# First keys' half of group 1 stored and loaded apart, slot by slot over two queues; first queries and constant rows over GpSimd's queue

## The reference

```
proj = quant4(x) @ ternary(Wqkv).T + b         # one projection for q, k and v
q = proj as (token, head, 16);  k = v = proj as (head, token, 16)
q, k = rotary(q), rotary(k)
ql, kl = q @ U, k @ U                          # U is 16 x 32
y  = softmax(ql @ kl.T / 4) @ v
x  = layernorm(x + quant4(y) @ ternary(Wo).T)
h  = silu(x @ w1.T * s1) * (x @ w2.T * s2)     # 256 -> 1024
h  = gelu(h @ h1.T * hs1);  h = gelu(h @ h2.T * hs2)
out = layernorm(x + h @ w3.T * s3)
```

## Time and profile before

| | |
|---|---|
| median of 3 runs | 2631.76 us |
| the profiled execution's own time | 2628.7 us |
| its span, first to last instruction | 2626.8 us |
| TensorE busy (matmul) | 2517.5 us, 96% |
| ScalarE busy | 2018.0 us, 77% |
| VectorE busy | 1735.6 us, 66% |
| GpSimd busy | 32.3 us, 1% |
| mean granted TensorE clock | 0.985 of full speed |
| DMA: moved, mean rate | 172.34 MB, 66 GB/s |
| first scores of attention start | 77.67 us |

### The profile page before, as it was taken

How to read it: one execution, slowest core, us unless ns; L and a number is a source line. 1 busy time by engine, 2 the same in 40 slices (tenths; PEclk the granted TensorE clock), 3 DMA queues, 4 the chain that set the end, 5 groups by cost and what they waited for, 6 DMA issues and landing times.

```text
span 2626.8 us, 41383 instructions
## 1 busy us (share of the span) xinstructions
PE 2517.5 (96%) x15898; PEld 1095.5 (42%) x15898; DVE 1735.6 (66%) x2465; ACT 2018.0 (77%) x2234; POOL 32.3 (1%) x64
## 2 busy tenths in 40 slices
PE   3799999999999999999999999999959999999998
PEld 2232222222222222222222222222238888888886
DVE  7354335887788788777877877877244656556563
ACT  2799999999999999999999999999932222222232
POOL 0000001200000000000000000000100000000000
PEclk8899999999999999999999999999979999999999
DMA  3544448833343333333333434323610001110000
GB/s 103 97 104 95 110 110 167 166 64 69 60 78 66 72 69 58 73 73 65 65 70 58 77 67 72 67 60 70 121 44 9 19 6 24 24 24 8 16 8 17
DMA packets 99992, 172.34 MB, mean 66 GB/s; under 512 B 30897, under 2 KB 56529, under 8 KB 99809
## 3 DMA queue, kind: packets, MB, share of 16 engines
q1 hardware_dynamic: 89304, 151.88, 28.8%
q0 software_dynamic: 8640, 15.73, 3.0%
q10 hardware_dynamic: 1864, 2.28, 0.4%
HBM read 144.34 MB, written 25.49 MB: 65 GB/s over the span
## 4 chain that ended last, share of the span: by engine, by line
PE 82%; ACT 7%; issue 5%; DVE 3%; DMA 2%; SPq 1%; ACTq 0%; DVEq 0%; POOLq 0%
PE PS L697 31%; PE PS L667 22%; PE PS L1052 18%; ACT PB L745 6%; PE PS L1037 5%; PE PS L1064 2%; PE PS L682 2%; ACT EXP L745 1%; PE PS L456 1%; PE PS L452 1%; DMA KSL<-KSD 0%; DVE yq L781 0%; DVE same L783 0%; DMA wh1r<-in_mlp 0%; PE PS L1026 0%
## 5 line engine op out<-in xcount | busy, mean ns | idle before, releaser
L745 ACT ACTIVATE PB<-PS 128x1024 f32<-128x1024 f32 x1856 | 1735.1, 1156 | 47.2 <-PE PS L667 44.4
L697 PE MATMUL PS<-PB,V 128*17 128x512 f32 x7424 | 977.8, 598 | 2.8 <-DVE accS L810 1.8
L667 PE MATMUL PS<-QSL,KSL 49*128 49x512 f32 x3904 | 840.5, 470 | 31.6 <-DMA KSL<-KSD 18.3
L667 PEld LDWEIGHTS PS<-QSL,KSL 49*128 49x128 f32 x3904 | 352.1, 184 | 951.5 <-ACT PB L745 856.0
L768 DVE SCALAR_TENSOR_TENSOR EXP<-EXP 128x1024 f32<-128x1024 f32 x288 | 352.8, 1225 | 9.9
L1127 ACT ACTIVATE hfr<-PS,s 128x512 f32<-128x512 f32 x128 | 86.8, 689 | 300.5 <-PE PS L1052 300.4
L697 PEld LDWEIGHTS PS<-PB,V 128*17 128x17 f32 x7424 | 123.1, 95 | 281.9 <-issue 217.2
L1052 PE MATMUL PS<-hidden_ar,wh1r 128*128 128x512 f32 x1024 | 237.5, 391 | 0.0
L756 DVE TENSOR_SCALAR EXP<-PS 128x512 f32<-128x512 f32 x192 | 132.6, 691 | 157.3 <-PE PS L682 154.9
L1052 PE MATMUL PS<-hidden_br,wh2r 128*128 128x512 f32 x1024 | 235.3, 390 | 0.0
L1052 PEld LDWEIGHTS PS<-hidden_br,wh2r 128*128 128x128 f32 x1024 | 191.7, 188 | 39.4
(11 more groups left out here) (149 smaller groups left out, 1455.9 us busy)
## 6 DMA issues: line engine op xcount, KB each, us to landing
KSL<-KSD SPq DMA_DIRECT2D x254, 256.0 KB
KSL<-KSD SPq DMA_DIRECT2D x254, 128.0 KB
QSL<-QSD SPq DMA_DIRECT2D x64, 132.0 KB
QSD<-qhl SPq DMA_DIRECT2D x32, 256.0 KB
wh2r<-in_mlp POOLq DMA_DIRECT2D x32, 256.0 KB, 4.3
KSD<-khl SPq DMA_DIRECT2D x60, 128.0 KB
xg<-in_x SPq DMA_DIRECT2D x8, 512.0 KB, 6.7
QSL<-QSD SPq DMA_DIRECT2D x64, 64.0 KB
```

The source lines that it names most:

```text
L667: ins = pe.matmul(PS[:, 2 * (pair % SLOTS) + e, :], KSL[r, q % 2, s, k * P:(k + 1) * P], QSL[r, b % 2, s, :], start=True, stop=True, tile_ ...
L697: ins = pe.matmul(ACC[i * VW:i * VW + DK + 1, :], V17[:, HT * h + u, c, :], probs[:, (i % 2) * QW:(i % 2 + 1) * QW], start=kt == 0, stop=k ...
L745: act.activation(probs, PS[:, slot:slot + 2, :].rearrange("p a b -> p (a b)"), ACT.Exp).then_inc(at["probs_ready"], 1)
```

## The change

It splits the first half of group 1's keys (keys 0 to 2047 of its two heads, which pieces 0 and 1 need) from the rest. It has a semaphore of its own, `k_first`. SP and ScalarE each store their part of this half, wait for all four of these stores, load their `e` of piece 0, store their part of the second half, and load their `e` of piece 1. So each slot is now filled by both queues, where before SP filled slot 0 and ScalarE slot 1. GpSimd loads the first queries, stores the constant rows of block 0, waits for them and loads the constants of both slots. The first scores of the two first pieces wait for `consts_first`, the first for `q_first`, and the counts on `k_in` and `q_in` are lowered to match. SP's load of piece 2 waits for the second half's stores as well.

```diff
         def first_scores_pe(pe, at, pair):
...
             if s == 0 and k == 0:
                 pe.wait_ge(at["k_in"][q % 2], keys_in(at, 0, q))
-            if s == 0 and kt == 0:
-                pe.wait_ge(at["q_in"][b % 2], (b // 2 + 1) * 64)
+                if q < 2:
+                    pe.wait_ge(consts_first[q], 32)
+            if unit == 0 and s == 0:
+                pe.wait_ge(q_first, 64)
+            elif s == 0 and kt == 0:
+                pe.wait_ge(at["q_in"][b % 2], (b // 2 + b % 2) * 64)
...
+        def keys_stored(eng, g):
+            if g == 1:
+                eng.wait_ge(k_first, 64)
+            eng.wait_ge(k_out[g], 64 if g == 1 else 128)
...
-        def store_keys(eng, g, p):
+        def store_keys(eng, g, p, halves=(0, 1)):
-            for half in range(2):
+            for half in halves:
                 for u in range(2):
                     eng.dma_start(KSD[2 * g + u, (1 - p) * DK:(2 - p) * DK, half * (N // 2):(half + 1) * (N // 2)].rearrange(
-                        "f (c k) -> c f k", c=8), khl[:, p, half, u * 256:(u + 1) * 256].bitcast(F32)).then_inc(k_out[g], 16)
+                        "f (c k) -> c f k", c=8), khl[:, p, half, u * 256:(u + 1) * 256].bitcast(F32)).then_inc(
+                            k_first if (g, half) == (1, 0) else k_out[g], 16)
...
-                for p in range(int(g == 1), 2):
-                    store_keys(sp, g, p)
+                if g == 1:
+                    store_keys(sp, g, 1, (0,))
+                else:
+                    for p in range(2):
+                        store_keys(sp, g, p)
...
+        def first_keys(eng, e):
+            eng.wait_ge(k_out[0], 128)
+            eng.wait_ge(k_first, 64)
+            load_keys(eng, first, 0, (e,))
+            store_keys(eng, 1, 1 - e, (1,))
+            load_keys(eng, first, 1, (e,))
...
         def _(sp):
...
                 if v == (KG, 1, 1):
-                    sp.wait_ge(q_out[0], 64)
-                    sp.wait_ge(qn_out[0], 16)
-                    load_queries(sp, first, 0, 0)
-                if v == (KM, 0, 1):
-                    sp.wait_ge(consts_out[0], 16)
-                    load_consts(sp, first, 0)
-                    for g in range(2):
-                        sp.wait_ge(k_out[g], 128)
-                    load_keys(sp, first, 0)
+                    first_keys(sp, 0)
...
         def _(pool):
+            pool.wait_ge(q_out[0], 64)
+            pool.wait_ge(qn_out[0], 16)
+            load_queries(pool, first, 0, 0, q_first)
+            pool.wait_ge(consts_ready, 1)
+            store_consts(pool, 0)
+            pool.wait_ge(consts_out[0], 16)
+            for q in range(2):
+                load_consts(pool, q, consts_first[q])
...
         def _(act):
...
                 if v == (KG, 1, 1):
-                    store_keys(act, 1, 0)
-            act.wait_ge(consts_out[0], 16)
-            load_consts(act, first, 1)
-            for g in range(2):
-                act.wait_ge(k_out[g], 128)
-            load_keys(act, first, 1)
+                    store_keys(act, 1, 0, (0,))
+                    first_keys(act, 1)
```

More of the change, by code:

```diff
@@ L238, in postln_block @@
         consts_ready, dve_s = sem("consts_ready"), sem("dve_s")
+        k_first, q_first, consts_first = sem("k_first"), sem("q_first"), [sem(f"consts_first{k}") for k in range(2)]
         q_out, k_out = [sem(f"q_out{g}") for g in range(NQ)], [sem(f"k_out{g}") for g in range(NQ)]
@@ L303, in keys_in @@
             if at is first:
-                return b * 160 + (96 if k < 2 else 160)
+                return b * 160 + (96 if k < 2 else 160) - 32
             return n0 * (QPB * 32) + (q // 2 + 1) * 64
@@ L371, in postln_block, with load_keys @@
         y_rows = a["y"].rearrange("(n r) (q c) -> n (r q) c", n=NB_ALL, c=H * DK)
-        def load_keys(sp, at, q):
+        def load_keys(sp, at, q, rows=(0, 1)):
             hb, k = divmod(q % (NBLK * QPB), QPB)
             ks = KSD.rearrange("(s e) r k -> e r s k", e=2)
-            for e in range(2):
+            for e in rows:
                 for r0, r1, to in ((0, 2 * DK, 0), (DK, 2 * DK, 2 * DK)):
@@ L465, in setup_pe, with stored_before @@
             ins.then_inc(setup_full, 1)
+        def keys_stored(eng, g):
+            if g == 1:
+                eng.wait_ge(k_first, 64)
+            eng.wait_ge(k_out[g], 64 if g == 1 else 128)
+        def stored_before(eng, what, g):
+            if what == KG:
+                keys_stored(eng, g - 1)
+            else:
+                eng.wait_ge(q_out[g - 1], 64)
         def setup_act(act, what, i, g):
@@ L481, in setup_act @@
                 else:
-                    hl, high, out, count = (khl, k_high, k_out, 128) if what == KG else (qhl, q_high, q_out, 64)
+                    hl, high = (khl, k_high) if what == KG else (qhl, q_high)
                     if i == 0 and g:
-                        act.wait_ge(out[g - 1], count)
+                        stored_before(act, what, g)
                     act.copy(hl[:, 0, i, :], bank).then_inc(high, 1)
@@ L585, in setup_dve @@
             elif what in (KG, QT_):
-                hl, high, out, count = (khl, k_high, k_out, 128) if what == KG else (qhl, q_high, q_out, 64)
+                hl, high = (khl, k_high) if what == KG else (qhl, q_high)
                 v.wait_ge(setup_full, use + 1)
                 if i == 0 and g:
-                    v.wait_ge(out[g - 1], count)
+                    stored_before(v, what, g)
                     v.wait_ge(k_abs if what == KG else q_abs, g)
@@ L647, in store_setup, with store_consts @@
                 b = g // 2
+                if b == 0:
+                    return
                 sp.wait_ge(consts_ready, b + 1)
[L649 to L650 removed]
+                store_consts(sp, b)
+        def store_consts(eng, b):
+            eng.dma_start(KSD[BL * b:BL * b + BL, 2 * DK:2 * DK + 1, 0:KEYS].rearrange("h a k -> (h a) k"),
+                          kcr[BL * b:BL * b + BL, :].bitcast(F32)).then_inc(consts_out[b], 16)
         x_rows = a["x"].rearrange("(t p) d -> p t d", p=P)
```

18 lines of the change are left out of this document (10 added, 8 removed).

## The result

The changed kernel takes 2620.94 us (median of 6 runs, 2618.33 to 2622.76) against 2630.53 us (6 runs, 2628.06 to 2632.18) before: a ratio of 0.9964, with a 95% interval of 0.9951 to 0.9977. That is 9.6 us less; 11.2 were forecast. The profiled execution took 2621.84 us with a span of 2619.7, where the one of before took 2628.7 with 2626.8.

The account below looks back on a forecast made before the run. TensorE's 18.3 us wait for keys was taken to set the start, and so the end. Latest of keys 64.1, projections 66.2, constants 64.4, plus 0.3: 66.5 instead of 77.67, 11.2 less, from 2630.2 to 2619.0 us; range 2614.5 to 2625.

Parts of the forecast that it names:

- T0: Start of the first scores: 66.5 us forecast instead of 77.67, the latest of keys, projections and constants plus release.
- Step (1): First-half key stores, two each on SP and ScalarE: all four landed at 58.5 us, bounds 57.7 to 62.8.
- Step (3): ScalarE's copy of group 2 behind six DMAs (3.8 us): starts at 62.4, projections read at 66.2; expected late next.
- The copy's tail: From the start of ScalarE's copy through TensorE's two projections to the end of VectorE's reading: 3.77 us.
- Steps (2) and (4): Slot 0's keys, alone at both queues' head, in by 64.1 us; GpSimd's chain of queries and constants by 64.4.
- Step (5): New waits after the start: slot 1 and second stores covered; group 2's rotated keys covered by less than 2 us.
- rival D: After T0, group 2's rotated keys or next copy late by 1 to 3 us: 2620 to 2622; chance 0.05.
- A: GpSimd's chain of queries and constants ends last: T0 72.3, gain 5.4, 2624.8 us; chance 0.13.
- B: Second stores and slot 1 share the DMA engines with slot 0: T0 71.5, 2624 us; chance 0.08.
- C: VectorE's work holds up GpSimd and its DMAs: T0 70.4, 2623 us; chance 0.04.
- E: GpSimd takes up a DMA only when the one before has landed: slower, 2634 or 2642.3 us; chance 0.04.
- F: First scores wait on something hidden behind the keys, T0 hardly moves: 2628 to 2631 us; chance 0.02.

Follow-up runs that it names:

- e1: The changed kernel with ScalarE's copy of group 2's transposed x ahead of its key DMAs: 2619.1 us, ratio 0.9962 to the kernel before.
- e2: The changed kernel with GpSimd loading the first queries only after the first stores landed, constant rows stored ahead of them: 2622.5 us, ratio 0.9969.
- e4: The key split alone, against the changed kernel: queries and slot 0's constants on SP behind its key DMAs, slot 1's constants on ScalarE: 2628.3 us, ratio 0.9993.
- e5: e1 with block 0's constant rows sent straight from SBUF into the key slots by eight GpSimd DMAs: 2617.6 us, ratio 0.9953.
- e6: e5 with GpSimd loading group 0's keys for both slots early, SP and ScalarE loading only group 1's part: 2617.9 us, ratio 0.9950.
- e7: e6 with ScalarE's two loads of slot 1 moved to SP's queue: 2615.9 us, ratio 0.9942.
- e3: GpSimd's part of the change alone (queries, constants), keys stored and loaded whole as in the kernel before: 2629.0 us, ratio 0.9996.
- e8: e7 with the first queries sent straight from SBUF by sixteen small DMAs in place of four query loads: 2619.1 us, ratio 0.9954.

## Why the prediction was right, and where its terms were off

**The mechanism.** The start sets the end, the half's split shortens the stores, slot 0 has a head start over slot 1, and ScalarE's copy of group 2 is late next: all four hold, the last by the chain and by e1. The forecast was 2619.0 us in a range of 2614.5 to 2625, and 2620.9 was measured. T0 was forecast at 66.5 and came at 69.7, outside the 65 to 69 that the prediction named as its sign of being right. That the time came nearer than T0 is luck. T0 moved by 8.0 us and not by 11.2, and by the prediction's own sum (2630.2 less what T0 gains) that gives 2622.2; the medians happen to lie 9.6 us apart where the two profiles lie 6.9 apart. The 3.2 us of T0 are three terms, less 0.2 for the release (0.3 forecast, 0.06 measured):

- **Step (1), the landing of the first stores: 58.5 forecast, 60.6 measured, 2.1 us.** The stores take as long as forecast when the queries do not flow beside them (58.54 in e2, 58.11 in e4). The step allowed the queries some tenths by adding their bytes to a mean rate. The stretches of the two profiles (columns as in the earlier trace rows), after and then e2:

```profile
54.00:58.00 4.00, 1.69 (x11) 0.87 (x10) 1.60 (x3) 0.00 (x0) 2.61 (x5) 0.57 0.51 124
58.00:60.50 2.50, 0.00 (x0) 0.00 (x0) 0.00 (x0) 0.00 (x0) 0.00 (x0) 0.50 0.54 185
```

```profile
54.00:58.50 4.50, 1.77 (x11) 0.98 (x11) 1.58 (x3) 0.13 (x1) 0.65 (x1) 0.63 0.40 122
```

Without the queries 0.55 MB move in 4.5 us, which is the stores and little else. With them 0.92 MB are asked for, yet the first four us move 0.50 MB, at the same rate, and the rest follows at 185 GB/s: the queries' bytes come in place of the stores'. The DMA engines were busy only 0.51 and 0.54 of these stretches, so it was not that all of them were full; what set the rate is open. Nor is it fixed: e5, with queries beside the stores too, moved 176 GB/s from 54 to 58 us and had its key loads out at 59.43.

- **Step (3), ScalarE's six DMAs: 3.8 us forecast, 5.0 measured.** The chain above has them one by one. Five cost 0.38 to 0.87 us, as the rows had it, but the last took 1.87 where such a load took 0.4 to 0.5 in the kernel before. e6 and e7 show more of it (3.57 us for two, 5.12 for four). It is no fixed addition: ScalarE issues the same six DMAs in 3.9 us in e1 (60.38 to 64.31), in 4.2 in e4, 4.4 in e2 and 5.3 in e5. The forecast met the lowest of these. The rows of before held no key loads issued right behind stores on the same queue; whether that is the cause is not shown.

- **The copy's tail: 3.77 us forecast, 3.94 measured** (65.69 to 69.63), with TensorE's projection at half clock throughout.

**Steps (2) and (4) were not last, but were optimistic too.** Slot 0's keys took 6.85 us from issue to use in e5, not 5.5. The row came from mid-kernel, where no second slot was asked for right behind; that this is the cause is likely, not shown. GpSimd's issues cost 0.5 to 0.68 us each, less than the 1.0 taken, and its trips more: the constants' store landed after 4.2 us (3.1 taken) and their loads after 5.5 in the median (2.9 taken), so that they were in at about 67.4, not at 64.4. The DMA issues of the changed kernel, KB each and median us to landing:

```profile
KSL<-KSD POOLq DMA_DIRECT2D x4, 8.0 KB, 5.5
KSD<-kcr POOLq DMA_DIRECT2D x1, 16.0 KB, 4.2
```

Had the copy not been in the way, T0 would have been 67.7 (e1), not 64.4 or 66.5.

**Step (5), what follows the start.** The loads of slot 1 and x were covered as forecast: no wait of TensorE for keys follows T0 up to 200 us, and the reading of x begins 17.4 us after T0 (87.06). The forecast took the loss after T0 as nothing; by the two profiles it is 0.7 us from the first exponential to unit 166 (343.0 against 342.3). The stretches show the granted clock. Before:

```profile
85.00:86.00 1.00, 1.00 (x10) 0.13 (x8) 0.64 (x1) 0.83 (x1) 0.00 (x0) 0.91 0.00 0
```

After:

```profile
77.00:78.00 1.00, 1.00 (x8) 0.41 (x10) 0.31 (x1) 1.00 (x2) 0.00 (x0) 0.50 0.00 0
78.00:79.00 1.00, 1.00 (x10) 0.03 (x2) 0.39 (x1) 0.16 (x1) 0.00 (x0) 0.78 0.00 0
```

Half speed is 1.2 GHz and full speed 2.4. By the shares 0.91 and 0.78 of these slices, each of which begins at half speed, full speed was granted at about 85.2 before, 7.5 us after T0, and at about 78.4 after, 8.7 us behind T0. TensorE was busy in both slices, and 1.2 us more at half speed are worth up to 0.6 of the 0.7 us, an estimate. VectorE's rotated keys of group 2 were ready at 74.7 and used at 76.54, so rival D's cause did not arise. Over the table the same stretch varies by 1.3 us without order, so the 0.7 us are more likely scatter than a cost of the change.

**The rivals.** A (GpSimd last) did not come true, though by 2 us only; in e1 and e2, where the copy or the queries were moved, GpSimd's constants do end the chain, and in e4 the constants are last on SP's queue. B (no head start for slot 0) fell: the first scores started 7.34 us after the key loads' issue in e1 and 6.85 in e5, with 1.3 MB of second stores and slot 1 behind it on the same queues, where both slots at once took 12.8 in e3. C fell: no DMA of GpSimd took longer to issue than 0.68 us beside VectorE's work. So the Trainium skill's rule (SBUF — State Buffer, "SBUF: two separate sides"), by which VectorE in a 2-port mode holds up such DMAs, is not seen in this trace; whether VectorE was in such a mode then, the rows do not tell. E fell: GpSimd's four query loads were issued in 2.48 us, with landings of 3.1 to 5.5 us, so it does not wait for one before the next. F fell, since T0 moved by 8.0 us.

The other rule that was weighed is the Trainium skill's (DMA: Bandwidth & Descriptors, "Issuing engines are not separate DMA queues"). Its first half, that the DMAs of all issuing engines interleave on the same DMA engines, agrees with step (1), where queries on GpSimd's queue slow stores on the other two. The second half, that issuing on several saves only issue time, may give too little here. e4, with the split and without the third queue, starts 6.9 us later than the changed kernel: the constants' store was not only issued 7.8 us later (64.66 against 56.88) but then took 8.3 us to land instead of 4.2. By then, though, it had the traffic of both slots beside it as well as the keys ahead of it on its queue, and no run parts the two.

## What to carry over to other kernels

When several conditions release the same instruction, list when each ends and what each edit puts behind it: here two parts, in the forms tried, brought 1 us of start each alone and 8 together. An engine that computes and also issues DMAs pays for each issue, here 0.4 to 2.2 us; put the computation that somebody waits for ahead of them (e1), and leave no issue on it when its next work is due (e7). Ahead of a wait on a transfer, count what else flows: queries that could not be used yet cost the stores 1 to 2.5 us. But moving such a transfer back is no gain by itself: in e2 the queries and the constants behind them then landed among the keys, and came last.

## What the runs showed that was not expected

The issue of a DMA on SP's or ScalarE's queue is not a fixed price. The same load of the key slots cost 0.4 to 0.6 us in the kernel before and in e3, where eight were issued at once, but 1.87 us in the changed kernel, 2.18 in e5, and 2.11 and 1.43 for loads of half the size in e6, each time behind earlier loads and stores of its queue. It is not the amount on its way alone: e3 had both slots asked for, too, and e7 and e8 issue the same four loads in 5.12 and 2.89 us. What limits it was not tried.

Small DMAs on GpSimd's queue slowed SP's issues (6.39 us for eight stores in e8, where the nine other kernels have 5.29 to 5.35) though they carried only 0.4 MB.

Twice as many bytes are not twice the time to land: half of slot 0 took 4.3 us in e6 and 4.0 in e7, and the whole 6.85 in e5, so that by a straight line, an estimate, 1.1 to 1.7 us are there whatever the size.
